# Two more chunks at either end of the first layer transposed through DRAM instead of on TensorE

## The reference

```python
def L0(x):       # 4 x 64 rows in the original's names; an adapter (LoRA) chosen by itok_B_2_6 for each batch
    gate = lora_add(einsum('bnh,fh->bnf', x, W_gate), x, A_gate, B_gate)   # 1376 columns
    up   = lora_add(einsum('bnh,fh->bnf', x, W_up),   x, A_up,   B_up)
    act  = silu(gate) * up
    return lora_add(einsum('bnf,hf->bnh', act, W_down), act, A_down, B_down)
x = x + L0(x)
x = x + L1(x)    # a 32 x 32 matrix for each batch, picked by itok_B_0_15
x = x + L2(x)    # base matmul 512 x 512, 8 experts of rank 16, top 2 by a router
x = x + L3(x)    # as L1 with other weights
```

## Time and profile before

| | |
|---|---|
| runs | 552.66, 552.68, 553.83 us; median 552.68 |
| the profiled execution | 554.27 us, of which the span of the trace is 552.4 |
| busy share of the span | PE 98%, VectorE (DVE) 60%, ScalarE (ACT) 38%, POOL 38% |
| granted clock of TensorE | 0.999 |
| the chain that ended last | PE 89%, DMA 5%, DVE 3%, ACT 1%, POOL 1% |

### The profile page before, as it was taken

One profiled execution on the slowest core, in us unless ns is written; L12 is line 12 of the kernel. 1 busy time (PEld: TensorE's weight loads), 2 busy tenths in 40 slices (PEclk: granted clock), 3 DMA queues, 4 the chain that ended last, 5 costly groups with the idle time before them and its releaser, 6 DMA issues.

```text
span 552.4 us, 8713 instructions
## 1 busy us (share of the span) xinstructions
PE 539.1 (98%) x3124; PEld 487.8 (88%) x3124; DVE 330.7 (60%) x781; ACT 209.2 (38%) x416; POOL 212.7 (38%) x236
## 2 busy tenths in 40 slices
PE   5989998999999999999999999999999999999997
PEld 5779987999989898989898989898989899999996
DVE  5798365564556555554545454545554577777765
ACT  6675232333342334242424242323333443444442
POOL 5743144647485758433323232232322232122100
PEclk9999999999999999999999999999999999999999
DMA  8976337566676767655564646555555832676742
GB/s 285 372 209 225 115 121 212 158 214 195 209 217 192 209 194 222 200 197 178 162 193 149 190 152 187 151 187 160 178 164 173 306 113 80 218 220 218 234 140 77
DMA packets 72027, 104.67 MB, mean 190 GB/s; under 512 B 9392, under 2 KB 39728, under 8 KB 71984
## 3 DMA queue, kind: packets, MB, share of 16 engines
q1 hardware_dynamic: 60960, 66.82, 36.9%
q0 software_dynamic: 10880, 37.23, 22.2%
q10 hardware_dynamic: 144, 0.06, 0.0%
HBM read 77.87 MB, written 26.21 MB: 188 GB/s over the span
## 4 chain that ended last, share of the span: by engine, by line
PE 89%; DMA 5%; DVE 3%; ACT 1%; POOL 1%; issue 1%; SPq 0%; DVEq 0%; ACTq 0%
PE gu_ps L1387 13%; PE gu_ps L1389 13%; PE gu_ps L1388 13%; PE down_ps L1387 8%; PE down_ps L1388 8%; PE down_ps L1389 8%; PE l_ps L1387 5%; PE l_ps L1388 5%; PE l_ps L1389 5%; PE gu_ps L1394 3%; PE gu_ps L1395 3%; DMA b_sel_raw<-b_gu,idx_rank 3%; DMA x_res<-act_blocks 2%; DVE b_sel L1121 1%; POOL a_raw L801 1%; PE down_ps L1395 1%
## 5 line engine op out<-in xcount | busy, mean ns | idle before, releaser
L1387 PE MATMUL down_ps<-wd_sb,act_hl 128*128 128x288 f32 (+1 forms) x352 | 104.0, 295 | 1.7 <-DVE act_hl L1121 1.5
L801 POOL DMA_INDIRECT b_sel_raw<-b_gu,idx_rank x48 | 48.1, 1003 | 148.9 <-PE gu_ps L1395 137.0
L1388 PE MATMUL down_ps<-wd_sb,act_hl 128*128 128x288 f32 (+1 forms) x352 | 103.7, 295 | 0.0
L1389 PE MATMUL down_ps<-wd_sb,act_hl 128*128 128x288 f32 (+1 forms) x352 | 103.6, 294 | 0.0
L1387 PE MATMUL gu_ps<-w_sb,xt 128*128 128x512 f32 x256 | 100.8, 394 | 0.0
L1389 PE MATMUL gu_ps<-w_sb,xt 128*128 128x512 f32 x256 | 100.0, 391 | 0.0
L1388 PE MATMUL gu_ps<-w_sb,xt 128*128 128x512 f32 x256 | 100.0, 391 | 0.0
L801 POOL DMA_INDIRECT a_raw<-a_all,idx_batch x60 | 70.5, 1175 | 59.9 <-DVE wd_sb L1121 45.9
L924 ACT ACTIVATE act<-gu_ps 128x512 f32<-128x512 f32 (+1 forms) x47 | 26.1, 555 | 174.1 <-PE gu_ps L1395 174.0
L1194 DVE TENSOR_TENSOR act<-act,gu_ps 128x512 f32<-128x512 f32 (+1 forms) x47 | 29.7, 633 | 102.4 <-ACT act L924 102.4
L1387 PEld LDWEIGHTS down_ps<-wd_sb,act_hl 128*128 128x128 f32 (+1 forms) x352 | 66.0, 188 | 4.0 <-DVE act_hl L1121 2.2
(11 more groups left out here) (162 smaller groups left out, 1053.1 us busy)
## 6 DMA issues: line engine op xcount, KB each, us to landing
act_blocks<-act SPq DMA_DIRECT2D x39, 256.0 KB, 4.1
x_res<-act_blocks SPq DMA_DIRECT2D x156, 64.0 KB
xt_raw<-x_t SPq DMA_DIRECT2D x16, 256.0 KB, 4.8
w_sb_raw<-wgu SPq DMA_DIRECT2D x16, 256.0 KB, 7.7
x_res<-x_rows SPq DMA_DIRECT2D x16, 256.0 KB, 3.8
x_after_l<-x_res SPq DMA_DIRECT2D x16, 256.0 KB, 2.2
bd<-bd_hl SPq DMA_DIRECT2D x16, 256.0 KB, 2.4
x<-x_after_l SPq DMA_DIRECT2D x16, 256.0 KB, 2.9
```

Source lines behind the costliest of these rows:

```text
L801: nc.gpsimd.indirect_dma_start(out=dst, out_offset=None, in_=table, in_offset=bass.IndirectOffsetOnAxis(ap=idx, axis=0)).then_inc(s, 16)
L1387: pe.matmul(out_, stationary[0], moving[0], start=start, stop=False, skip_group_check=True)
L1388: pe.matmul(out_, stationary[0], moving[1], start=False, stop=False, skip_group_check=True)
L1389: return pe.matmul(out_, stationary[1], moving[0], start=False, stop=stop, skip_group_check=True)
```

## The change

- `MOVED` becomes 4 to 46: chunks 4, 5 (tile 1) and 45, 46 (tile 15) are no longer transposed on PE. Chunk 47 still is.
- All residual tiles use `x_res[:, 0]`; the store of tile 1 is no longer in front of the first moved chunk. The waits of the first one change accordingly.
- `move_act(s - 1)` goes up in SP's loop, ahead of the w2ra, block-diagonal and b2 loads at steps 46 and 47.
- The lo of act 45 goes to step 47's list (ahead of gate 47), that of act 46 to step 48's list (first). `down(45)` is issued from the loop, at the same place as before; `down(46)` stands where it stood.
- `down(4)` moves behind `up(6)`, `down(5)` to the end of step 7; the down adapters and x1 of tile 1 move from step 7 to step 8.
- For tiles 0 and 1, t is transposed on PE (`transpose_t`, two 128x128 transposes each) and copied by ScalarE ("tc"), in place of the chain in VectorE. Around it lists are reordered: t 0 ahead of b 1, the last gather of tile 0's down factors behind b 2, `x_a(1)` into the middle of `gate(3)`, the first half of `gate(4)` ahead of `adapters(2)`.

```diff
-MOVED = range(FREE, STEPS - 3)
+MOVED = range(4, STEPS - 1)
...
-        return {-1: a_items(0, 0) + [("b", 0), ("b", 1)] + a_items(1) + a_items(0, 1),
-                0: [("b", 2)],
+        return {-1: a_items(0, 0) + [("b", 0), ("b", 1)] + a_items(1) + a_items(0, 1)[:-1],
+                0: [("b", 2)] + a_items(0, 1)[-1:],
...
-                0: (wgu_items(1, 0) + [("at", 0)] + w1u[:2] + [("b", 0), w1u[2], ("tm", 0), w1u[3], ("b", 1), ("t", 0),
-                    ("at", 1), w2g[0], ("gate", 0)]),
-                1: w2g[1:] + [("gate", 1), ("tm", 1)] + wgu_items(2, 1) + [("t", 1)],
+                0: (wgu_items(1, 0) + [("at", 0)] + w1u[:2] + [("b", 0), w1u[2], ("tm", 0), w1u[3], ("t", 0), ("b", 1),
+                    ("tc", 0), w2g[0], ("gate", 0), w2g[1], ("at", 1)]),
+                1: w2g[2:] + [("gate", 1), ("tm", 1)] + w2u[:2] + [("t", 1)] + w2u[2:] + [("tc", 1)],
...
-                6: [("act", 4), ("tm", 2), ("act", 5), ("t", 2), ("adt", 2), ("bd", 1), ("tdm", 1), ("gate", 6),
-                    ("b", 7)]}[s]
+                6: [("act", 4), ("tm", 2), ("t", 2), ("adt", 2), ("gate", 6), ("b", 7)]}[s]
...
     if i == NT:
-        return last + [("bd", i - 1), ("tdm", i - 1), ("td", i - 1), ("x1", i - 1)]
+        return [("act", s - 2)] + last + [("bd", i - 1), ("tdm", i - 1), ("td", i - 1), ("x1", i - 1)]
...
                 if d - 1 in MOVED:
                     sp.wait_ge(s_lo, s_lo_of(("act", d - 1)))
                 else:
-                    store_tile(1)
-                    sp.wait_ge(s_xout[1], 16)
+                    sp.wait_ge(s_actt, pe_transposed(down_no(2)))
...
                     load_tile(0)
                     load_tile(1)
+                if s - 1 in MOVED:
+                    move_act(s - 1)
                 if s == STEPS - 2:
                     sp.wait_ge(s_gu, chunk_done(0))
...
                 if s == 5:
                     store_tile(0)
-                    sp.wait_ge(s_actt, down_no(2) + 1)
-                    sp.dma_start(x_res[:, 1, :], x_rows[P:2 * P, :]).then_inc(s_xin[1], 16)
-                if s - 1 in MOVED:
-                    move_act(s - 1)
+                    sp.wait_ge(s_xout[0], 16)
+                    sp.dma_start(x_res[:, 0, :], x_rows[P:2 * P, :]).then_inc(s_xin[1], 16)
...
+                if kind == "tc":
+                    i = job[1]
+                    sc.wait_ge(s_tt, i + 1)
+                    sc.copy(t_hl[:, i, :, :], t_ps[:, i, :, :]).then_inc(s_tc, 1)
+                    return
...
                     masked.append(job)
+                    if i < EARLY_T:
+                        lo(t_rows[:, :, :, 1, :], masked_t(), t_rows[:, :, :, 0, :]).then_inc(s_lo, 1)
+                        return
                     turn(lo(t_rows[:, :, :, 1, :], masked_t(), t_rows[:, :, :, 0, :]))
...
             x_a(0)
-            up(1, 0, HC // 2)
-            up(1, HC // 2, HC)
+            up(1, 0, HC - 1)
+            transpose_t(0)
+            up(1, HC - 1, HC)
             adapters(0)
             adapters(1)
+            gate(3, 0, HC // 2)
             x_a(1)
-            whole(gate, 3)
+            gate(3, HC // 2, HC)
             transpose_act(0)
-            whole(up, 3)
+            up(3, 0, HC // 2)
+            transpose_t(1)
+            up(3, HC // 2, HC)
+            gate(4, 0, HC // 2)
             adapters(2)
-            gate(4, 0, HC // 2)
             adapters(3)
...
-            transpose_act(4)
             whole(gate, 6)
+            whole(up, 6)
             down(4)
-            transpose_act(5)
-            whole(up, 6)
-            down(5)
             adapters(6)
             for s in range(FREE + 1, STEPS):
                 i, n = ORDER[s]
-                finishes = n == (1 if i == 2 else 2)
+                finishes = n == 2
...
-            down(STEPS - 3)
             down(STEPS - 2)
             transpose_act(STEPS - 1)
```

More of the change, by code:

```diff
@@ L231, in lane_jobs @@
     if s <= FREE:
[L232 removed]
+        w1u, w2g, w2u = wgu_items(1, 1), wgu_items(2, 0), wgu_items(2, 1)
         return {-1: first_items(),
[L234 to L236 removed]
+                0: (wgu_items(1, 0) + [("at", 0)] + w1u[:2] + [("b", 0), w1u[2], ("tm", 0), w1u[3], ("t", 0), ("b", 1),
+                    ("tc", 0), w2g[0], ("gate", 0), w2g[1], ("at", 1)]),
+                1: w2g[2:] + [("gate", 1), ("tm", 1)] + w2u[:2] + [("t", 1)] + w2u[2:] + [("tc", 1)],
                 2: [("b", 2), ("adt", 0), ("b", 3), ("adt", 1), ("gate", 2), ("act", 0)] + wd_items(0),
@@ L249, in lane_jobs @@
         return [("tm", i)] + acts + [("t", i), ("gate", s), ("b", s + 1)]
-    if n == 1 and i == 2:
-        return [("td", i - 1), ("x1", i - 1), ("x", i + 1, 0), ("gate", s), ("b", s + 1)]
     if n == 1:
@@ L254, in lane_jobs @@
         return acts + x + [("bd", i - 1), ("gate", s), ("tdm", i - 1), ("b", s + 1), ("td", i - 1)]
-    jobs = acts[:1] + [("x1", i - 1)] + acts[1:] if i > 2 else acts
+    jobs = acts[:1] + [("x1", i - 1)] + acts[1:]
     if i + 1 < NT:
@@ L258, in lane_jobs @@
     return jobs + [("gate", s)]
-NO_SPLIT = ("gate", "tm", "tdm", "x1")
+NO_SPLIT = ("gate", "tm", "tc", "tdm", "x1")
+EARLY_T = 2
 def bass_conditioned_residual_chain(nc, x_t, x_rows, it_cond, it_lang, wgu, wd, a_all, a_gu, a_d, b_d,
@@ L353, in bass_conditioned_residual_chain @@
         act_t = ps("act_t", [HC, P], banks_a)
-        spare_ps = ps("spare_ps", [HC, P], banks_a)
+        t_ps = ps("t_ps", [EARLY_T, 2, P], banks_a)
         banks_a.close()
@@ L445, in bass_conditioned_residual_chain @@
         s_turn = sem("s_turn")
+        s_tt = sem("s_tt")
+        s_tc = sem("s_tc")
         s_gu = sem("s_gu")
@@ L655, in store_tile @@
                 sp.wait_ge(s_x1, i + 1)
-                sp.dma_start(x_scratch[i * P:(i + 1) * P, :], x_res[:, res_slot(i), :]).then_inc(s_xout[i % 2], 16)
+                sp.dma_start(x_scratch[i * P:(i + 1) * P, :], x_res[:, 0, :]).then_inc(s_xout[i % 2], 16)
             def load(it):
@@ L752, in _ @@
                     i, n = ORDER[s]
-                    if n == 2 and i > 2:
+                    if n == 2:
                         store_tile(i - 1)
[L755 to L758, removed]
+                        sp.wait_ge(s_xout[(i - 1) % 2], 16 * ((i - 1) // 2 + 1))
+                        sp.dma_start(x_res[:, 0, :], x_rows[i * P:(i + 1) * P, :]).then_inc(s_xin[i % 2], 16)
             def store_x2(t):
@@ L959, in job_hi @@
                         sc.wait_ge(s_lo, s_lo_of(("t", i - 1)))
+                    if 1 <= i <= EARLY_T:
+                        sc.wait_ge(s_tt, i)
                     hi(t_rows[:, :, :, 0, :], masked_t())
@@ L1114, in tile_indices @@
                 ve.wait_ge(s_const2, 32)
+                ve.wait_ge(s_tt, EARLY_T)
                 pick(1, "is_ch", TB)
@@ L1160, in blocks @@
                 if s == MOVED[0]:
-                    ve.wait_ge(s_actt, s)
+                    ve.wait_ge(s_actt, pe_transposed(down_no(3)))
                 else:
@@ L1186, in job_lo @@
                     ve.wait_ge(s_dl, i + 1)
-                    x_i = x_res[:, res_slot(i), :].rearrange("p (j n) -> p j n", n=HALF)
+                    x_i = x_res[:, 0, :].rearrange("p (j n) -> p j n", n=HALF)
                     ve.tensor_tensor(x_i, x_i, base_cols(i), ALU.add).then_inc(s_x1, 1)
@@ L1436, in adapters @@
                 if n == 0:
-                    pe.wait_ge(s_lo, s_lo_of(("t", i)))
+                    pe.wait_ge(*((s_tc, i + 1) if i < EARLY_T else (s_lo, s_lo_of(("t", i)))))
                 for m in range(2):
@@ L1441, in adapters, with transpose_t @@
                 mm.then_inc(s_gu, 1)
+            def transpose_t(i):
+                pe.wait_ge(s_lo, s_lo_of(("t", i)))
+                if i == 0:
+                    pe.wait_ge(s_ident, 16)
+                for m in range(2):
+                    mm = pe.transpose(t_ps[:, i, m, :],
+                                      t_rows[:, m, :, :, :].bitcast(F32).rearrange("p b d r -> p (b d r)"), ident)
+                mm.then_inc(s_tt, 1)
             def transpose_act(d):
```

2 lines of the change are left out of this document (removed).

## The result

The changed kernel is **slower**, by 0.6%: 556.86 us, the median of 8 runs (555.55 to 558.87), against 553.62 for the kernel before, also of 8 runs (552.66 to 554.22). The ratio is 1.0058, interval [1.0046, 1.0071]. In two of the three sessions of experiments all kernels scatter over some 12 us, that of before too (553.6 to 566.5, and 553.5 to 565.8), and its longer runs there have the lower mean granted clock (the twelve at 1.000 took 553.5 to 558.2, the eleven at 0.988 or less 561.2 to 566.5), so that a median there can't tell 2 us. The direction forecast as the likelier one came true, but 556.86 lies 1.3 us above the range. Part of that is the base: the three runs of before that were known had their median 0.94 lower than the eight; from 553.62 the forecast would have been 554.7 and the range's end 556.5, still short.

The account below looks back on a forecast made before the run. The prediction took PE, busy for 98% of the span, as the bound. Its terms -1.65 - 2.0 - 0.2 + 4.9 = +1.05 us on the median of 552.68 gave 553.7 us, range 551.0 to 555.6.

Parts of the forecast that it names:

- part 2: Stalls of PE at chunks 6 and 7 vanish once tile 1's store is not in front: -2.0 us.
- part 1: Act transposes of chunks 4, 5, 45 and 46 removed from PE: -1.65 us.
- part 3: Start of the layer: down(0) earlier, the gain limited at adapters(3) by the gather of b 3: -0.2 us.
- The term for t: Start: t by PE and ACT makes adapters(0) 1.2 us earlier, but only 0.2 us remains at adapters(3).
- Part 4: End of the layer: chunk 45's round trip delays the loads for L2, causing two PE waits: +4.9 us.
- S: First PE wait at the end, before l1(0), behind POOL's late low_x1(0): 2.8 to 4.2 us, taken as 3.2.
- The wait before down(46): Second PE wait at the end, for act 46's lo late in DVE's list: 1.5 us, whatever S is.
- The clock: Rival at the end: TensorE's clock falls with the wait, 1.4 us more; chance 0.10.
- Nothing counted: End: b2 load, block diagonals 3 to 7 and residual rows some 10 us later, PE 4.9 later; no cost.
- the loads for L2 are early enough: Rival at the end: w2ra lands early enough, S is 0, the end costs 1.6 us, total 550.4; chance 0.18.
- the start keeps its lead: Rival at the start: b 3 lands 1 us earlier, part 3 is -1.2 us, total 552.7; chance 0.10.
- moved chunks 4 and 5 wait: Rival: chunks 4 and 5 wait as 6 and 7 did, up to 1.5 us more, 555.2; chance 0.08.

Follow-up runs that it names:

- filler: Changed kernel plus twelve 512-column matmuls on PE ahead of l1(0)'s wait, their results overwritten; 562.36 us, ratio 1.0078.
- end_mended: Changed kernel with low_x1(0) before unit_w2, block diagonals before w2ra, act 46 split behind gate 47, tile 2's residual row loaded before the store wait; 555.70 us, ratio 1.0035.
- start_again: Same kernel as start_only, timed on another occasion; 554.24 us, ratio 0.9996.
- start_only: Only the change's start on the kernel before: chunks 45 and 46 stay on PE, SP's old list at the end; 556.46 us, ratio 0.9963.
- only_45_ahead: Changed kernel with chunk 46 transposed on PE again; chunk 45's DRAM trip stays ahead of the loads for L2; 561.68 us in one run.
- old_t: The change's start with the old end, but t of tiles 0 and 1 by VectorE's chain as in the kernel before; 557.19 us in one run.
- end_only: Only the change's end on the kernel before's start: chunks 45 and 46 moved, trips ahead of the loads for L2; 565.95 us, ratio 1.0118.
- start_more: Same kernel as start_only, timed once more; 559.55 us, ratio 1.0023.
- only_45_behind: Changed kernel with chunk 46 transposed on PE again and chunk 45's trip behind the loads of w2ra and block diagonals 0 to 2; 560.91 us, ratio 1.0042.

## Why the prediction was wrong

**Parts 1 to 3** hold by their sum. The transposes are gone, and after has no wait of PE between 39 and 430 us, as part 2 had it. From the silu of gate 3 to that of gate 45 it is 387.53 us before and 384.65 after: -2.88, which is part 1's share there and part 2 (0.88 + 2.0). Of part 3: down(0) came at 38.50 instead of 38.66, and adapters(3) waited 0.74 where I expected 1.9. The -0.17 at the silu of gate 3 looks like the forecast 0.2, but that is luck as far as is known: PE's first matmul starts 0.29 earlier in after (5.45 for 5.74), which no part of the change explains. The four traces with this start and no wait of PE in the middle from after's and the second session have the silu of gate 45 at 422.86 to 423.33, 2.9 to 3.4 earlier. The term for t by itself stays untested.

**Part 4 (+4.9, with the transposes of the end +4.1)** measured +7.45. Its mechanism was right twice. S, the wait before l1(0) released by POOL, was 2.85 with 0.15 of restart (I had 3.2); on before's clock l1(0) starts at 444.3, in the 443.1 to 444.5 forecast, and PE comes to it 1.1 later than forecast because of down(44). The wait before down(46) cost 1.5 (I had 1.5). Taking back one order at a time removed the second and halved the first. The step that failed is the one that closed the sum there. Three terms were missing:
- *The clock, 1.7.* It stood as a rival with 0.10 and "Waits of 1.3 us in the trace cost no clock; one of 3 us isn't in it." Between the two I chose the end that the trace didn't show; the size (1.4) was nearly right. The rule of the Trainium skill, "TensorE: Matmul & The Clock Gate", Part 1, that idleness closes the gate, is what this trace does; filler shows it.
- *"Nothing counted", 1.0.* The store and load of residual rows, 10 us later, were set against PE's being later by 4.9. But the load of tile 2 waits for tile 14's store, which took 6 us behind the block diagonals (446.76 to 452.77 on SP), and ACT's order put td of tile 15 and x1(3) behind it.
- *down(44), 1.1.* The forecast has nothing for it. What the record shows is that SP issued the loads of act 44 in 3.07 us instead of 1.91 and that they landed late; by filler, end_mended and start_again this isn't bound to the moved chunk 45, and its cause stays open.

4.1 + 1.7 + 1.0 + 1.1 = 7.9, less 0.4 for S and the restarts and 0.1 for transposes that were worth more, is 7.4 of 7.45. The rival "the loads for L2 are early enough" fell, as did "the start keeps its lead" and "moved chunks 4 and 5 wait". The range ended too early because it added the clock to the forecast's middle and not to its upper bound, though both hang on the same wait: a long S is what makes the clock fall. Nor is its end the sum of the two cases that it names: 553.7 + 1.4 + 1.5 is 556.6, not 555.6.

## What to carry to other kernels

Before work is moved from the bounding engine to a trip through DRAM, write down for its last instances what stands behind each of its DMAs in the issuing queue and who needs that, and the other way round what it would stand behind: here ahead cost 4.7 us at one consumer, behind made the store take 6.5 to 6.9 us instead of 3.7 and stopped an engine that wanted the buffer back. The same change cut to its start, with the last chunks left on PE, is the part worth having by its trace; its shortest runs (550.2 to 551.1) lie below all of both kernels, but no session shows its median clearly below that of before, so that a gain isn't shown by the medians. And a new wait of TensorE of nearly 3 us is to be priced with the half-speed stretch behind it in the main sum.

## What was not expected of the hardware

The clock fell after each wait of 2.59 us or more that I read in the last step (2.59, 2.74, 2.85, 3.13), and stayed after those of 1.41, 1.43 and 1.72. Elsewhere it is the same: it fell with the waits of 2.85, 2.88, 3.65 and 3.76 at 157 to 166 us (start_only, end_mended, only_45_ahead, old_t) and of 2.96, 3.30, 3.44 and 4.26 at 21 to 26 us (end_only, start_only, start_more, only_45_behind), and it stayed after one of 1.75 (start_only, 196.06). But a fall doesn't need a long wait. In filler's trace it falls between 22 and 23 us with no wait over 0.5 near it: PE was busy for 0.33, 0.61 and 0.51 of the three microseconds from 20 on. In end_only it fell only after PE had worked again: l1(0) started at 447.13, the next starts followed at 0.34, 0.23 and 0.24, and only from 447.94 on they were 0.38 to 0.43 apart, until 451.30.

The granted clock and the pace don't agree at the very start of the trace. Before's matmuls of 352 columns start 0.30 apart up to 8.5 us, as the prediction reads the earlier trace rows, and 0.16 later; the profile gives a granted clock of 1.00 for all of 5 to 9 us. There the low level is read from the pace alone.

A store of 256 KB landed after 3.7 us in the middle of the layer and after 6.5, 6.9 and 6.9 where the loads for L2 had been issued just before it: its size is the same, and the traces differ in what was issued in front of it. That this sets the time is the plain reading; no run varied it alone.
